# Key and value sums of the projections stage: every second chunk, two chunks together

## The chip, the cores and the metric

The kernel runs on one core of one Trainium2 chip. The metric is the device time of one execution in microseconds (us). Before the change the median of three runs is 2619.73 us (2617.83 to 2623.37).

A core has several engines that run at once and wait for one another through counters (semaphores): TensorE (PE) multiplies matrices, VectorE (DVE) and ScalarE (ACT) work on elements and empty TensorE's results, GpSimd (POOL) works on elements too, SyncE (SP) issues transfers (DMA).

## The reference

The input is 8 images of 256 channels and 64 x 64 positions. Two residual layers follow one another, each behind a group norm:

```python
x = x + window_mixing(group_norm(x))           # 8x8 windows, 16 heads
x = x + attention(group_norm(x))

def attention(x):                              # 256 channels, groups of 8
    qkv  = w_qkv @ x                           # 768 x 256, at each position
    y    = grouped_1x1(depthwise_5x5(qkv))
    q, k, v = heads(concat(qkv, y))            # q = relu(q), k = relu(k)
    v    = pad_with_ones(v)                    # a ninth row, for the denominator
    vk   = sum over positions of v * k         # per image and head: 9 x 8
    out  = (vk @ q)[:8] / ((vk @ q)[8] + 1e-15)
    return batch_norm(w_proj @ out)
```

The change touches the sum `vk` for the heads that come straight from `qkv`, before any convolution.

## The kernel before

The kernel has four stages, one after the other, with a barrier of all engines between them: window mixing, projections, convolved heads, output. The change is in `projections`.

**What a chunk is.** The stage goes through the 8 images; each image is cut into 8 chunks of 512 positions (`n` from 0 to 7), so there are 64 chunks. For each chunk TensorE makes six products `product(b, n, j)` (line 1056). Each is one block of 128 of the 768 output channels, and six matmuls, since operands are split into a high and a low part (`xh`, `xl`, `wh`, `wl`). The products write three PSUM banks in turn (`o_ps`). Products 0 and 2 are blocks of keys, which ACT copies to `kv` (line 976); 1 and 3 are values, copied to `kv` by DVE (line 1201); 4 and 5 are queries, copied to `qw` by ACT (line 1004) and DVE (line 1236).

**Turning and summing.** For the sum over positions, positions must lie on the partitions. `turn(b, n, u)` transposes the key and value tiles of half `u` on TensorE (line 1070), ACT takes the result into `kT` and `vT` (lines 981 and 984), and `sum_vk(b, n, u)` (line 1082) multiplies them: 16 small matmuls of 128 x 32 by 33 columns, each of which the trace shows as two, so 32 for a half and 64 for a chunk. They add up in the bank `vk_ps` over all 8 chunks of an image. The 64 of a chunk stand at its very end, behind product 5; I call them a burst.

**What else TensorE waits for.** The first matmul of a chunk waits for the split of the chunk's input: ACT normalises (`xn`, line 907) and rounds to `xh` (line 917), DVE subtracts to `xl` (line 1148). It also waits for the copies that free its banks. DVE's order in a chunk is: copy of values, two subtractions for the stores (lines 1154 to 1160), those of the queries of the chunk before, second copy of values, two more subtractions, the split `xl` for the next chunk, the copy of queries (line 1236). In chunks 1 to 4 of all images but the last it then adds the statistics of the next image (line 111); after chunk 4 it puts them together (line 120), and in chunk 5 TensorE averages them over groups, between products 1 and 2 (line 158).

**Stores.** DVE and POOL write the differences and the odd columns to `stage`, and SP stores it: six transfers of 408 KB and two of 256 KB a chunk. `stage` has two sets by chunk. At the end of an image ACT starts the load of the image after next, 4096 KB.

**Order in the code.** Each engine runs its own program. `over_image_pairs` writes images 0 and 1 out, runs a loop twice over images 2 to 5, and writes images 6 and 7 out. In the loop, the values of waits are computed in registers; in the written-out code they are constants.

Of the kernel before, what the change touches and what calls it, by code (L numbers as in the profile page):

```python
# [29 lines left out]
P = 128  # L30
# [30 lines left out]
SQ = 32  # L61
# [610 lines left out]
def projections(nc, K, x1_dram, qkv_dram, qr_dram, w_pw, bn_in, taps_dram, sorted_dram):  # L672
# [3 lines left out]
    with ExitStack() as ctx:  # L676
# [21 lines left out]

        kv = sb("kv", [P, 2, 4, 512])
        qw = sb("qw", [P, 2, 2, 512])  # L700
        kT = sb("kT", [P, 2, 4, P])
        vT = sb("vT", [P, 2, 4, NSQ, VS])
        tick = sb("ptick", [P, 4 * NCH])
        pw_rep = sb("pw_rep", [P, QT, NPH, D])
        diag = sb("pdiag", [P, 2, SQ])
# [119 lines left out]

        @block.gpsimd
        def _(pool):
            pool.memset(vT[:, :, :, :, SQ:VS], 1.0).then_inc(zeroed, 1)

            def body(i, last_body):  # L830
                for par in range(2):
                    b = 2 * i + par

                    def pause(k, n):

                        k = NCH * k + n
                        pool.tensor_tensor(tick[:, k:k + 1], K["ident"][:, 0:1], K["ident"][:, 1:2], ALU.add)  # L837

                    def border(n):

                        row = NB * (1 - n // 4)
                        keys_values_free(pool, b, n)
                        queries_free(pool, b, n)
                        pause(0, n)
                        pool.memset(stage[:, n % 2, :, :, :, row, :].rearrange("p t a k x -> p (t a) k x"), 0.0)\
                            .then_inc(bordered, 1)

                    def edge(buf, t0, j0, n):

                        if n % 2:  # L850
                            pool.tensor_scalar(staged(j0, n, 0, 0, 1), every_second(buf, t0, n, 0, 1), -1.0, None, ALU.mult)
                        else:
                            pool.tensor_copy(staged(j0, n, 1, HALF - 1, HALF), every_second(buf, t0, n, NB - 1, 1))

                    def keys_values(n, u):
                        g = NCH * b + n
                        pool.wait_ge(kv_ready, 2 * g + u + 1)
                        pool.wait_ge(kv_ready_v, 2 * g + u + 1)
                        keys_values_free(pool, b, n)
                        pause(1 + u, n)  # L860
                        edge(kv, 2 * u, 2 * u, n)
                        pool.tensor_copy(staged(2 * u, n, 2), every_second(kv, 2 * u, n, 1 - n % 2)).then_inc(kv_odd, 1)

                    def queries(n, end=False):
                        g = NCH * b + n
                        pool.wait_ge(q_ready, g + 1)
                        pool.wait_ge(q_ready_v, g + 1)
                        queries_free(pool, b, n)
                        at_least(pool, K["qr_stored"][n % 2], 32 * (4 * b + n // 2))
                        pause(3, n)  # L870
                        edge(qw, 0, 4, n)
                        pool.tensor_copy(staged(4, n, 2), every_second(qw, 0, n, 1 - n % 2)).then_inc(q_odd, 1)
                        if end:
                            return
                        for t in range(2):
                            last = pool.tensor_scalar(qs[:, n % 2, t, :], qw[:, n % 2, t, :], 0.0, None, ALU.max)  # L876
                        last.then_inc(qs_ready, 1)

                    for n in range(NCH):
                        if n % 4 < 2:  # L880
                            border(n)
                        keys_values(n, 0)
                        if n > 0:
                            queries(n - 1)
                        keys_values(n, 1)
                    queries(NCH - 1, last_body and par == 1)
            over_image_pairs(pool, body)

        @block.scalar
        def _(act):  # L890
# [72 lines left out]
            def body(i, last_body):  # L963
                for par in range(2):
                    b = 2 * i + par
                    for n in range(NCH):
# [10 lines left out]

                        def turned(u):
                            act.wait_ge(t_full, 4 * g + 2 * u + 1)
                            at_least(act, vk_full, g)  # L980
                            act.activation(kT[:, u, :, :].rearrange("p a c -> p (a c)"), t_ps[:, 0, :], ACT.Relu)\
                                .then_inc(k_turned, 1)
                            act.wait_ge(t_full, 4 * g + 2 * u + 2)
                            act.activation(vT[:, u, :, :, 0:SQ].rearrange("p a q c -> p (a q) c"),
                                           t_ps[:, 1, :].rearrange("p (a c) -> p a c", c=SQ), ACT.Copy).then_inc(v_turned, 1)
                        key(0)
                        if last_body and par == 1 and n == 0:
# [35 lines left out]
        def _(pe):  # L1023
# [50 lines left out]
            def sum_vk(b, n, u):  # L1074
                pe.wait_ge(k_turned, 2 * (NCH * b + n) + u + 1)
                pe.wait_ge(v_turned, 2 * (NCH * b + n) + u + 1)
                if n == 0:
                    at_least(pe, vk_taken, 2 * b)
                for a in range(4):
                    for q in range(NSQ):  # L1080
                        ch = slice(SQ * q, SQ * q + SQ)
                        last = pe.matmul(vk_ps[ch, u, 0:VS], kT[:, u, a, ch], vT[:, u, a, q, :],
                                         start=(n == 0 and a == 0), stop=(n == NCH - 1 and a == 3))
                if u == 1:
                    last.then_inc(vk_full, 1)

            def turn_pointwise(step):
# [8 lines left out]
            def body(i, last_body):  # L1096
                for par in range(2):
                    b = 2 * i + par
                    for n in range(NCH):
                        pe.wait_ge(xh_ready, NCH * b + n + 1)  # L1100
                        pe.wait_ge(xl_ready, NCH * b + n + 1)
                        means = variances = None
                        if n == 5 and not (last_body and par == 1):
                            means, variances = norm_group_sums(pe, b + 1, T, mv, stat_ps, K["gavg"], ns)
                        product(b, n, 0)
                        product(b, n, 1)
                        if means:
                            means()
                        product(b, n, 2)
                        turn(b, n, 0)  # L1110
                        if last_body and par == 1 and n in (0, NCH - 1):
                            turn_pointwise(n // (NCH - 1))
                        product(b, n, 3)
                        product(b, n, 4)
                        if variances:
                            variances()
                        turn(b, n, 1)
                        product(b, n, 5)
                        for u in range(2):
                            sum_vk(b, n, u)  # L1120
            over_image_pairs(pe, body)

        @block.vector
        def _(dve):
# [64 lines left out]
            def body(i, last_body):  # L1189
                for par in range(2):  # L1190
# [56 lines left out]
                        if nxt and n == 6:  # L1247
                            scale()
                    queries(NCH - 1)
                    dve.wait_ge(vk_full, NCH * (b + 1))  # L1250
                    at = bass.ds(image(i, par), 1)
                    dve.tensor_tensor(diag[:, :, :], vk_ps[:, :, 0:SQ], K["sqmask"][:, :].unsqueeze(1).broadcast_to([P, 2, SQ]),
                                      ALU.mult).then_inc(vk_taken, 1)
# [903 lines left out]
```

## Time and profile before

| what | value |
|---|---|
| median of the runs | 2619.73 us |
| profiled execution, span from the first to the last instruction | 2613.5 us |
| its own time beside its span | not given apart; the median of the runs is 6.2 us above the span |
| PE busy over the whole span | 2464.0 us (94%) |
| DVE, ACT, POOL busy | 2045.9, 1577.8, 1133.2 us |
| projections stage, about | 366 to 1112 us |
| one chunk, in the written-out code and in the loop | 10.9 and 11.1 us, where nothing holds it up |

The span is cut into stages by their lines. Within the stage the timeline shows each instruction with its start and its duration. Matmuls are pipelined: their durations overlap, so the distance from start to start tells what one costs. An entry in square brackets is idle time of the engine before the instruction, with what ended it.

### The profile page before, as it was taken

Reading aid. Unit: us, or ns where it says so; the run is one execution under the profiler, and the core shown is the slowest. Engines: PE = TensorE matmul, PEld = TensorE weight load, DVE = VectorE, ACT = ScalarE, POOL = GpSimd, SP = SyncE. Lnnn points to the kernel's source line nnn. Section 1 sums busy time; section 2 is a strip of 40 time slices with the busy share of each in tenths; the row PEclk is TensorE's granted clock in tenths of the full one; section 3 lists DMA queues with packets and bytes.
Section 4 is the critical chain, followed back from the end, with each engine's and each line's share of the span. In section 5 each row is a group of like instructions: output and inputs, shape, how many; then the busy total and the mean of one; then the engine's idle time right before and its main releaser. Section 6 shows DMA issues by size and latency. Waiting matters only on the chain. (4 is left out here: it accounts for less than half of the span.)

```text
span 2613.5 us, 62159 instructions
## 1 busy us (share of the span) xinstructions
PE 2464.0 (94%) x22829; PEld 1891.7 (72%) x22829; DVE 2045.9 (78%) x2869; ACT 1577.8 (60%) x2144; POOL 1133.2 (43%) x1631
## 2 busy tenths in 40 slices
PE   5888889999999999979999999999999979999998
PEld 4666667777778778767777777777777746666665
DVE  7777668778877877788888888888888767887885
ACT  5888855666556666666666666666666534334343
POOL 7732327878768777800000000000000048888887
PEclk9999999999999999989999999999999989999999
DMA  7655238888888898998888888888888777777774
GB/s 264 254 199 209 110 113 306 324 321 290 314 311 292 294 334 301 302 243 205 200 199 204 199 199 204 200 199 205 199 198 204 207 241 280 281 277 272 262 270 129
DMA packets 300327, 628.28 MB, mean 240 GB/s; under 512 B 50656, under 2 KB 248032, under 8 KB 294752
## 3 DMA queue, kind: packets, MB, share of 16 engines
q1 hardware_dynamic: 295072, 590.90, 73.5%
q10 hardware_dynamic: 4048, 31.11, 3.3%
q0 software_dynamic: 1008, 3.67, 0.4%
q8 instruction: 118, 1.93, 0.3%
q14 instruction: 81, 0.66, 0.1%
HBM read 327.81 MB, written 300.94 MB: 241 GB/s over the span
## 5 line engine op out<-in xcount | busy, mean ns | idle before, releaser
L1834 POOL TENSOR_TENSOR ql<-image,qh 128x1024 fp32r<-128x1024 f32 x128 | 306.1, 2423 | 999.0 <-ACT qh L1862 999.0
L1490 PE MATMUL c_ps<-dh,wh 128*128 128x512 f32 x1152 | 474.1, 412 | 14.5 <-DVE wl L1640 13.2
L1402 ACT ACTIVATE dh<-image 128x1632 fp32r<-128x1632 f32 x192 | 301.3, 1569 | 277.8 <-PE c_ps L1490 261.2
L1490 PE MATMUL c_ps<-dh,wl 128*128 128x512 f32 x1152 | 454.1, 394 | 0.0
L1490 PE MATMUL c_ps<-dl,wh 128*128 128x512 f32 x1152 | 452.5, 393 | 0.0
L1598 DVE TENSOR_TENSOR dl<-image,dh 128x1632 fp32r<-128x1632 f32 x192 | 355.9, 1854 | 59.8 <-ACT dh L1402 59.8
L1056 PE MATMUL o_ps<-xh,wqh 128*128 128x512 f32 x768 | 320.3, 417 | 11.1 <-issue 7.9
L1056 PE MATMUL o_ps<-xl,wqh 128*128 128x512 f32 x768 | 304.4, 396 | 0.0
L1056 PE MATMUL o_ps<-xh,wql 128*128 128x512 f32 x768 | 303.1, 395 | 0.0
L1490 PEld LDWEIGHTS c_ps<-dh,wh 128*128 128x128 f32 x1152 | 217.0, 188 | 70.5 <-DVE wl L1640 13.3
L1490 PEld LDWEIGHTS c_ps<-dl,wh 128*128 128x128 f32 x1152 | 216.5, 188 | 51.8
L1490 PEld LDWEIGHTS c_ps<-dh,wl 128*128 128x128 f32 x1152 | 217.1, 188 | 40.2
L976 ACT ACTIVATE kv<-o_ps 128x512 f32<-128x512 f32 x128 | 76.8, 600 | 268.5 <-PE o_ps L1056 252.2
L876 POOL TENSOR_SCALAR qs<-qw 128x512 f32<-128x512 f32 x126 | 235.9, 1889 | 0.0
L1883 ACT ACTIVATE zs<-z_ps,bn_shift 128x512 f32<-128x512 f32 x64 | 44.0, 687 | 283.2 <-PE z_ps L1970 283.2
L1970 PE MATMUL z_ps<-qh,fh 128*128 128x512 f32 x512 | 208.7, 408 | 5.7 <-POOL ql L1834 4.0
L1970 PE MATMUL z_ps<-qh,fl 128*128 128x512 f32 x512 | 201.0, 393 | 0.0
L1970 PE MATMUL z_ps<-ql,fh 128*128 128x512 f32 x512 | 200.4, 392 | 0.0
L1201 DVE COPY kv<-o_ps 128x512 f32<-128x512 f32 x128 | 87.8, 686 | 123.9 <-PE o_ps L1056 121.9
L1056 PEld LDWEIGHTS o_ps<-xh,wqh 128*128 128x128 f32 x768 | 146.2, 190 | 39.7 <-issue 14.1
L837 POOL TENSOR_TENSOR ptick<-ident 128x1 f32<-128x1 f32 x224 | 93.4, 417 | 179.9 <-DMA qkv_scratch<-stage 77.2
L1056 PEld LDWEIGHTS o_ps<-xl,wqh 128*128 128x128 f32 x768 | 146.1, 190 | 32.6
(209 smaller groups left out, 5387.5 us busy)
## 6 DMA issues: line engine op xcount, KB each, us to landing
qkv_scratch<-stage SPq DMA_DIRECT2D x384, 408.0 KB, 4.1
image<-qkv_scratch SPq DMA_DIRECT2D x189, 816.0 KB, 6.3
qr_scratch<-qs SPq DMA_DIRECT2D x128, 256.0 KB, 3.2
yq_scratch<-qy SPq DMA_DIRECT2D x64, 512.0 KB, 6.8
image<-qr_scratch SPq DMA_DIRECT2D x128, 256.0 KB, 6.3
image<-yq_scratch SPq DMA_DIRECT2D x128, 256.0 KB, 5.7
ox<-x_scratch SPq DMA_DIRECT2D x8, 4096.0 KB, 15.1
out<-ox SPq DMA_DIRECT2D x7, 4096.0 KB, 12.7
```

The source lines that it names most:

```text
L837: pool.tensor_tensor(tick[:, k:k + 1], K["ident"][:, 0:1], K["ident"][:, 1:2], ALU.add)
L876: last = pool.tensor_scalar(qs[:, n % 2, t, :], qw[:, n % 2, t, :], 0.0, None, ALU.max)
L976: act.activation(kv[:, n % 2, 2 * u, :], o_ps[:, (2 * u) % 3, :], ACT.Copy).then_inc(kv_ready, 1)
L1056: last = pe.matmul(o_ps[:, j % 3, :], w[:, ct, P * t:P * t + P], xx[:, n % 2, ct, :], start=(k == 0), stop=(k == 5))
L1201: dve.tensor_copy(kv[:, n % 2, 2 * u + 1, :], o_ps[:, (2 * u + 1) % 3, :]).then_inc(kv_ready_v, 1)
L1402: act.activation(dh[kind][:, :], raw[kind], ACT.Copy).then_inc(hi_ready, 1)
L1490: last = pe.matmul(c_ps[:, bank(hp, j, kind, m), :], w[hp][:, kind, part, o:o + P], cells[:, :, HALF * dy:HALF * dy + HALF * NB], start=(k ...
L1598: dve.tensor_tensor(dl[kind][:, :], raw[kind], dh[kind][:, :].bitcast(F32), ALU.subtract)\
L1834: pool.tensor_tensor(two_of(ql, n, tp), two(n, tp), two_of(qh, n, tp).bitcast(F32), ALU.subtract)\
L1883: act.activation(zs[:, :], z_ps[:, 1, :], ACT.Identity, bias=bn["shift"][:, 1:2]).then_inc(z_taken, 1)
L1970: last = pe.matmul(z_ps[:, o, :], w[par][:, t, P * o:P * o + P], d, start=(m == 0), stop=(m == 3 * KT - 1))
```

## The change

`kT` and `vT` get a second set, picked by the chunk's parity (`n % 2`). TensorE leaves out the sums at the end of chunks 0, 2, 4 and 6, and does them at the end of chunks 1, 3, 5 and 7, for the chunk before and for the chunk itself: 128 small matmuls in a row. The counter `vk_full` goes up once for two chunks, and those who wait for it, ACT before it writes `kT` and DVE at the image's end, count accordingly. The amount of arithmetic is the same. The burst's place and size are all that moves on TensorE; ACT, DVE, POOL and SP keep their order.

```diff
-        kT = sb("kT", [P, 2, 4, P])
-        vT = sb("vT", [P, 2, 4, NSQ, VS])
+        kT = sb("kT", [P, 2, 2, 4, P])
+        vT = sb("vT", [P, 2, 2, 4, NSQ, VS])
...
-                            at_least(act, vk_full, g)
-                            act.activation(kT[:, u, :, :].rearrange("p a c -> p (a c)"), t_ps[:, 0, :], ACT.Relu)\
+                            at_least(act, vk_full, (NCH // 2) * b + n // 2)
+                            act.activation(kT[:, n % 2, u, :, :].rearrange("p a c -> p (a c)"), t_ps[:, 0, :], ACT.Relu)\
...
-                        last = pe.matmul(vk_ps[ch, u, 0:VS], kT[:, u, a, ch], vT[:, u, a, q, :],
+                        last = pe.matmul(vk_ps[ch, u, 0:VS], kT[:, n % 2, u, a, ch], vT[:, n % 2, u, a, q, :],
                                          start=(n == 0 and a == 0), stop=(n == NCH - 1 and a == 3))
-                if u == 1:
+                if u == 1 and n % 2 == 1:
                     last.then_inc(vk_full, 1)
...
                         product(b, n, 5)
-                        for u in range(2):
-                            sum_vk(b, n, u)
+                        if n % 2 == 1:
+                            for m in (n - 1, n):
+                                for u in range(2):
+                                    sum_vk(b, m, u)
...
-                    dve.wait_ge(vk_full, NCH * (b + 1))
+                    dve.wait_ge(vk_full, (NCH // 2) * (b + 1))
```

On TensorE, the end of chunk 2 of the first image and the start of chunk 3, in the kernel before (`xl_ready` is the split that DVE makes, `v_turned` and `k_turned` are ACT's copies):

```order
L1056 MATMUL o_ps<-xl,wqh 128x512
L1082 MATMUL vk_ps<-vT,kT 32x33 [waits v_turned,k_turned]
L1082 MATMUL vk_ps<-vT,kT 32x33 x15
L1082 MATMUL vk_ps<-vT,kT 32x33 [waits v_turned,k_turned]
L1082 MATMUL vk_ps<-vT,kT 32x33 x15
L1056 MATMUL o_ps<-xh,wqh 128x512 [waits kv_ready_v,q_ready,xl_ready,xh_ready]
```

The same place now:

```order
L1056 MATMUL o_ps<-xh,wqh 128x512
L1056 MATMUL o_ps<-xh,wql 128x512
L1056 MATMUL o_ps<-xl,wqh 128x512
L1056 MATMUL o_ps<-xh,wqh 128x512 [waits kv_ready_v,q_ready,xl_ready,xh_ready]
L1056 MATMUL o_ps<-xh,wql 128x512
```

The first matmul of chunk 3, with its wait for the split, follows product 5 of chunk 2 directly.

On TensorE, the end of chunk 3 now (it had the same rows as the end of chunk 2 before):

```order
L1056 MATMUL o_ps<-xl,wqh 128x512
L1082 MATMUL vk_ps<-vT,kT 32x33 [waits v_turned,k_turned]
L1082 MATMUL vk_ps<-vT,kT 32x33 x15
L1082 MATMUL vk_ps<-vT,kT 32x33 [waits v_turned,k_turned]
L1082 MATMUL vk_ps<-vT,kT 32x33 x15
L1082 MATMUL vk_ps<-vT,kT 32x33 [waits v_turned,k_turned]
L1082 MATMUL vk_ps<-vT,kT 32x33 x15
L1082 MATMUL vk_ps<-vT,kT 32x33 [waits v_turned,k_turned]
L1082 MATMUL vk_ps<-vT,kT 32x33 x15
```

The sums of two chunks stand in a row, with one switch from the large matmuls and one back.

## Rows read from the trace of the kernel before

**Rows 1.** Windows, projections stage: busy PE, PEld, DVE, ACT, POOL; clock, DMA, GB/s.
```profile
366.00:1112.00 746.00, 715.89 (x7458) 583.66 (x7458) 577.26 (x880) 454.65 (x658) 570.42 (x763) 0.98 0.86 302
```

**Rows 2.** Groups by line, projections stage, the sums (line 1082).
```profile
L1082 PE MATMUL vk_ps<-vT,kT 128*32 128x33 f32 x4096 | 49.9, 200 | 1.3 <-ACT vT L984 1.3
```

**Rows 3.** Timeline of PE, end of chunk 4, loop (start us, duration us, ...).
```profile
611.13 0.40 PE L1056 MATMUL o_ps<-xh,wql 128*128 128x512 f32 x1
611.36 0.40 PE L1056 MATMUL o_ps<-xl,wqh 128*128 128x512 f32 x1
611.69 0.77 PE L1082 MATMUL vk_ps<-vT,kT 128*32 128x33 f32 x64
...
612.61 0.47 PE L1056 MATMUL o_ps<-xh,wqh 128*128 128x512 f32 x1
612.91 0.39 PE L1056 MATMUL o_ps<-xh,wql 128*128 128x512 f32 x1
...
615.81 0.38 PE L158 MATMUL pstat_ps<-pmv,gavg 128*128 128x2 f32 x2 [0.24 <-DVE pmv L120]
```

**Rows 4.** Timeline of DVE beside Rows 3.
```profile
610.87 1.21 DVE L1148 TENSOR_TENSOR xl<-xn,xh 128x1024 fp32r<-128x1024 f32 x1
612.01 0.67 DVE L1236 COPY qw<-o_ps 128x512 f32<-128x512 f32 x1
612.61 2.45 DVE L111 BATCH_NORM_STATS2 pbst<-image 128x6 f32<-128x512 f32 x4
...
615.17 0.59 DVE L120 BATCH_NORM_AGGREGATE pmv<-pbst 128x2 f32<-128x48 f32 x2
```

**Rows 5.** Timeline of DVE and PE, end of a chunk 2, unrolled code.
```profile
497.94 1.22 DVE L1148 TENSOR_TENSOR xl<-xn,xh 128x1024 fp32r<-128x1024 f32 x1
...
498.56 0.39 PE L1056 MATMUL o_ps<-xl,wqh 128*128 128x512 f32 x1
...
499.60 0.47 PE L1056 MATMUL o_ps<-xh,wqh 128*128 128x512 f32 x1
```

**Rows 6.** Timeline of DVE and PE, end of a chunk 2, loop.
```profile
871.35 1.22 DVE L1148 TENSOR_TENSOR xl<-xn,xh 128x1024 fp32r<-128x1024 f32 x1
...
871.68 0.40 PE L1056 MATMUL o_ps<-xl,wqh 128*128 128x512 f32 x1
...
872.92 0.47 PE L1056 MATMUL o_ps<-xh,wqh 128*128 128x512 f32 x1
```

**Rows 7.** Timeline of DVE and PE, end of a chunk 0, loop.
```profile
844.82 1.22 DVE L1148 TENSOR_TENSOR xl<-xn,xh 128x1024 fp32r<-128x1024 f32 x1
...
845.57 0.40 PE L1056 MATMUL o_ps<-xl,wqh 128*128 128x512 f32 x1
```

**Rows 8.** Timeline, DVE and PE, chunk 1, the wait on stores.
```profile
853.80 0.63 DVE L1154 TENSOR_TENSOR stage<-kv 128x448 f32<-128x448 f32 x1 [3.08 <-DMA qkv_scratch<-stage]
...
856.91 1.48 PE L1070 MATMUL pt_ps<-ident,kv 128*128 128x128 f32 x8 [2.12 <-DVE kv L1201]
```

**Rows 9.** Timeline of ACT and PE, chunk 6 of the last image.
```profile
1097.13 0.59 ACT L1004 ACTIVATE qw<-o_ps 128x512 f32<-128x512 f32 x1
...
1098.85 0.46 PE L1082 MATMUL vk_ps<-vT,kT 128*32 128x33 f32 x32 [1.27 <-ACT vT L984]
1099.24 0.50 PE L1056 MATMUL o_ps<-xh,wqh 128*128 128x512 f32 x1
```

**Rows 10.** Timeline of DVE and SP's queue, end of the stage.
```profile
1113.88 0.22 DVE L1252 TENSOR_TENSOR pdiag<-vk_ps,sqmask 128x64 f32<-128x64 f32 x1
...
1115.92 2.30 SPq L798 DMA_DIRECT2D qr_scratch<-qs  x2
```

**Rows 11.** Timeline of DVE, the same subtraction twice in one chunk.
```profile
840.52 0.65 DVE L1160 TENSOR_TENSOR stage<-kv 128x448 f32<-128x448 f32 x1
...
843.80 1.10 DVE L1160 TENSOR_TENSOR stage<-kv 128x448 f32<-128x448 f32 x1
```

**Rows 12.** Timeline of PE, start of the loop's second turn.
```profile
743.93 0.77 PE L1056 MATMUL o_ps<-xh,wqh 128*128 128x512 f32 x1 [4.44 <-issue]
```

More of the change, by code:

```diff
@@ L827, in _ @@
         def _(pool):
-            pool.memset(vT[:, :, :, :, SQ:VS], 1.0).then_inc(zeroed, 1)
+            pool.memset(vT[:, :, :, :, :, SQ:VS].rearrange("p m u a q c -> p (m u a) q c"), 1.0).then_inc(zeroed, 1)
             def body(i, last_body):
@@ L979, in turned @@
                             act.wait_ge(t_full, 4 * g + 2 * u + 1)
-                            at_least(act, vk_full, g)
-                            act.activation(kT[:, u, :, :].rearrange("p a c -> p (a c)"), t_ps[:, 0, :], ACT.Relu)\
+                            at_least(act, vk_full, (NCH // 2) * b + n // 2)
+                            act.activation(kT[:, n % 2, u, :, :].rearrange("p a c -> p (a c)"), t_ps[:, 0, :], ACT.Relu)\
                                 .then_inc(k_turned, 1)
                             act.wait_ge(t_full, 4 * g + 2 * u + 2)
-                            act.activation(vT[:, u, :, :, 0:SQ].rearrange("p a q c -> p (a q) c"),
+                            act.activation(vT[:, n % 2, u, :, :, 0:SQ].rearrange("p a q c -> p (a q) c"),
                                            t_ps[:, 1, :].rearrange("p (a c) -> p a c", c=SQ), ACT.Copy).then_inc(v_turned, 1)
```

## The prediction

> **What bounds the kernel now.** I read the page first, for the stage that the change touches, then the stage by windows, then TensorE's timeline at the ends of chunks, and beside it DVE's. In the projections stage PE is busy 715.9 of 746 us, DVE 577.3, ACT 454.7, POOL 570.4, and the DMA share is 0.86 [rows 1]. So TensorE bounds the stage by its own work, and the reader should ask of each end of a chunk: if TensorE gets there earlier, what does it find ready?
>
> The burst of 64 sum matmuls costs little [rows 2, 3]. Matmuls of the products start 0.23 us apart (611.13 to 611.36). Product 5 ends its last start at 611.36, so without a burst the next product could start at 611.59. It starts at 612.61, and its second matmul follows after 0.30 instead of 0.23. The burst of chunk 4 in the loop thus costs 612.61 - 611.59 + 0.07 = 1.09 us. In code that is written out it costs less: 499.60 - (498.56 + 0.23) = 0.81, with the same slow start 0.88 [rows 5]. The difference of 0.2 lies behind the burst, where TensorE works out the values of its waits in registers with no matmul queued that would hide it. A burst takes 0.77 us from its first start to its last end, and one small matmul 0.20, so the 64 starts span 0.57; another 64 behind them cost 0.58. The other 0.30 (written out) or 0.51 (loop) is the way in and out.
>
> **What the change saves if nothing else is late.** 32 ways in and out go, 16 in each kind of code: 16 x 0.30 + 16 x 0.51 = 13.0 us. This is the optimistic sum, and I do not forecast it, since a second half of the change works against it: the burst at the end of an even chunk also covers the split that the next chunk needs.
>
> **What the burst covers.** DVE's split ends at 610.87 + 1.21 = 612.08 in chunk 4, 0.49 us behind the moment at which product 5 leaves TensorE free [rows 3, 4]. In a chunk 2 of the loop it is 871.35 + 1.22 = 872.57 against 871.68 + 0.23 = 871.91: late by 0.66 [rows 6]. In a written-out chunk 2 it is 499.16 against 498.79: late by 0.37 [rows 5]. Only in chunk 0 it is about in time, 846.04 against 845.80, late by 0.24 [rows 7]. DVE begins its series in each of these chunks when product 1 is done, so it moves with TensorE, and the lateness stays when the chunk shifts. Today 1.02 or 0.81 us of burst lie over it and it costs nothing. Without a burst TensorE waits for it, and then pays the hand-over (a few hundredths to 0.1 us, as in rows 3 and 4, where the group average starts 0.05 us after the statistics end at 615.76), in the loop also part of the register work, some 0.2.
>
> **The sum by place in the image.** Savings are in us over all 8 images.
> - Ends of chunks 1, 3 and 5 carry a second 64 matmuls. Nothing lies beside them but what is already waiting, so they are on the path: 24 x 0.58 = 13.9 slower. From below it could be 0.57 less a few hundredths, as the second half has no way in; from above a small matmul that is held up at a lower clock would make it about 0.9 in one or two of them. I take 0.58.
> - End of chunk 7 (+0.58, 7 times, the last image apart) and end of chunk 0 (saves 0.6 to 0.8 written out, about 0.95 in the loop, 7.0 in all) lie between the start of an image's load and the wait for stores that follows in chunk 1 or 2. There DVE waits 3.08 us for a store, and TensorE 2.12 us for DVE [rows 8]. That wait ends when the transfers are through, so what comes before it is given back. Six of eight images have one. Of 4.1 - 7.0 = -2.9 a quarter stays: -0.8. The ends of the range are 0 and -2.9.
> - End of chunk 2: loop 1.02 - 0.66 - 0.26 = 0.1, four times; written out 0.81 - 0.37 - 0.1 = 0.3 at most, three times, with 0.2 as the mean; in the first image, where the chunk follows the wait for stores, the whole 1.1. Together -2.1.
> - End of chunk 4: nothing in seven images. TensorE's next hold is the group average in chunk 5, which begins at 615.81 after 0.24 us of idling, and what it waits for is DVE's series of split, query copy, statistics and aggregation from 610.87 to 615.76 without a gap [rows 3, 4]. No part of that series waits for a burst. TensorE only comes to the wait earlier. The last image has no statistics: -0.3.
> - End of chunk 6: as chunk 2, 0.1 four times in the loop and about 0.3 three times outside: -1.4.
> - End of chunk 6 of the last image: the second half of the burst waited 1.27 us for ACT, which was issuing transfers [rows 9]. Now nothing waits there but product 0 of chunk 7, for ACT's query copy, which ends at 1097.13 + 0.59 = 1097.72. It can start at 1097.8 instead of 1099.24: -1.4.
> - End of chunk 7 of the last image: free. The stage's end goes over DVE's subtractions to SP's last transfers at 1115.92 + 2.30, and DVE takes up the sum only after them, at 1113.88 and without idle time in front [rows 10]; between product 5 and that point it copies, makes the batch norm's scale and two long subtractions, which covers 0.58.
> - ACT's wait before it writes `kT` now asks for the pairs done before the chunk; the last is half a chunk old when ACT gets there. POOL's and SP's order stays. Zero.
>
> Sum: 13.9 - 0.8 - 2.1 - 0.3 - 1.4 - 1.4 = 7.9 us slower. Against the profiled span of 2613.5 this is 2621.4; the median of the runs lies 6.2 above that span, and 2619.7 + 7.9 = 2627.6. As several of the small savings are taken at their lower bound, I put 2627.
>
> **The rule on switching.** The rows show 0.30 to 0.51 us around each burst that is not matmuls of the burst. The Trainium skill ("TensorEngine Tiling (Array Packing)", Key Properties) says that going from one tiling mode to another drains TensorE. Here the products use the whole array and the sums 32 columns of it, so the rule speaks for the change, and by it alone the time would be the optimistic one. The trace agrees that there is a cost at each switch; it does not say that TensorE would find its next input ready.
>
> **Rivals.**
> - *Faster: the split comes in time.* The switches go and TensorE does not wait, but for the average in chunk 5. Then 13.0 is saved less about 1.0 in each of seven chunks 4: -6, giving 2613.5. For it speaks that DVE's split is held back by other work that could shift: the same subtraction before it takes 1.10 us at 843.80 and 0.65 at 840.52 [rows 11]; if it were always the short one, the split would be 0.45 earlier, enough in most written-out chunks and in none of the chunks 2 of the loop (0.66 late). The point from which it decides is a split 0.5 us earlier than now. Against it: the relation of DVE to POOL within an even chunk is set by the same copies as before. The Trainium skill ("SBUF — State Buffer", Who interferes with whom) says that a DVE instruction with two SBUF inputs contends with a GpSimd instruction that reads SBUF, which is how such a shift would act; rows 11 agree with a cost of 0.45 us and cannot tell whose reads cause it.
> - *No change: the waits for stores take it all back.* If transfers set the pace over the whole image (share 0.86), each delay shortens the waits of rows 8, some 2 to 3 us in six images, which are enough for 7.9 in all. Then the time is 2621. Against it: the waits follow the load of 4096 KB and come at the start of an image; the stores of chunks 3 to 6 are through by then.
> - *Much slower: 128 matmuls in a row outrun the supply of instructions.* At the loop's turn TensorE idles 4.44 us for nothing but issue [rows 12]. If each double burst drew 0.5 us of that, 32 x 0.5 = 16 more: 2643. Against it: bursts of 64 show no such gap.
>
> **Chances.** Forecast 0.58, faster 0.12, no change 0.18, much slower or a knock-on late DVE 0.12. A change under 0.2% (5.2 us) cannot be told from none for this kernel. The forecast gives slower with 0.8 of its chance (0.46), as its sum could come out between 3 and 11; with 0.10 of the last rival that is 0.56. Faster is 0.12, and the rest, 0.32, is the same. The range reaches down to the rival without change and some way to the faster one, 2615, and up to a third of the way from the forecast to the last rival and a bit, 2634; about 1 in 10 lies outside on each side. The forecast's own range is 2622 to 2631.
>
> **What would show it.** In the changed profile: bursts of 128, 1.3 to 1.4 us from first start to last end; first products of chunks 3 and 7 of the loop 0.9 to 1.0 us behind product 5's end, with DVE's split named as what ended TensorE's idle time; chunk 5's average at the same distance from chunk 4's start; chunk 7 of the last image starting 1.4 us sooner after chunk 6. Wrong would be a first product that starts at once after chunks 2 and 6 (the faster rival), waits on stores that shrink by the growth of the chunks (the rival without change), or a burst well over 1.4 us (the slower one).

## The result, and the profile after

| kernel | median | lowest to highest | profiled span |
|---|---|---|---|
| before | 2622.09 us | 2617.83 to 2623.87 (5 runs) | 2613.5 us |
| changed | 2642.81 us | 2635.08 to 2645.38 (5 runs) | 2633.3 us |

The ratio is 1.0075, 95% interval [1.0061, 1.009]: 20.7 us slower between the medians, 19.8 between the spans. The forecast was 7.9 slower, and the time lies above the range, at the price of the last rival, 2643. One run of all, the second of the spread kernel's repeat below, was slow (2781.98 us at a granted clock of 0.845 against 0.984 in the first), and no reading uses it.

The projections stage took 757.1 us from its first product to the first convolution matmul of the next stage; now it takes 773.2. Of the 19.8 us these are 16.1; another 2.9 lie before the stage (last section) and 0.8 behind it. The answers to [rows 1, 2], and below them the weight loads and the first matmuls of the products, by lines (busy, mean ns, then idle time with its releasers):

```profile
366.00:1131.00 765.00, 713.07 (x7452) 583.05 (x7452) 580.36 (x885) 457.92 (x662) 569.06 (x764) 0.98 0.84 294
```

```profile
L1082 PE MATMUL vk_ps<-vT,kT 128*32 128x33 f32 x4096 | 46.0, 198 | 8.3 <-issue 8.3
...
L1056 PE MATMUL o_ps<-xh,wqh 128*128 128x512 f32 x768 | 320.3, 417 | 26.8 <-issue 14.1 <-DVE xl L1150 10.5 <-ACT qw L1004 0.7
```

The second line in the kernel before:

```profile
L1056 PE MATMUL o_ps<-xh,wqh 128*128 128x512 f32 x768 | 320.3, 417 | 11.1 <-issue 7.9 <-DVE xl L1148 0.6
```

TensorE is busy no longer than before. Two kinds of idling came: 10.5 us behind DVE's split, which is the end of the even chunks, and "issue": 8.3 us inside the bursts, which [rows 2] did not have, and 14.1 in front of the products, most of it behind bursts and at the loop's turn, where it was 7.9. The clock (0.98) and the DMA share (0.84, before 0.86) did not move against it.

**Ends of chunks that went as forecast.** TensorE's timeline at the end of a chunk 1 of the loop, which answers to [rows 3]:

```profile
776.26 0.39 PE L1056 MATMUL o_ps<-xl,wqh 128*128 128x512 f32 x1
776.57 1.39 PE L1082 MATMUL vk_ps<-vT,kT 128*32 128x33 f32 x128
778.16 0.47 PE L1056 MATMUL o_ps<-xh,wqh 128*128 128x512 f32 x1 [0.21 <-issue]
```

The burst of 128 spans 1.39 us, as forecast. The next, a chunk 2 of the loop, TensorE and DVE, which answers to [rows 6]:

```profile
788.06 0.40 PE L1056 MATMUL o_ps<-xl,wqh 128*128 128x512 f32 x1
789.28 0.47 PE L1056 MATMUL o_ps<-xh,wqh 128*128 128x512 f32 x1 [0.83 <-DVE xl L1150]
```

```profile
787.72 1.22 DVE L1150 TENSOR_TENSOR xl<-xn,xh 128x1024 fp32r<-128x1024 f32 x1
788.85 0.68 DVE L1238 COPY qw<-o_ps 128x512 f32<-128x512 f32 x1
```

The split ends at 788.94, 0.65 us behind 788.29, when TensorE was free (forecast 0.66), and the product follows 0.99 behind that point. The burst that lay over it before cost 1.02: nothing is gained. A chunk 4, TensorE, which answers to [rows 3] in the same place:

```profile
614.62 0.40 PE L1056 MATMUL o_ps<-xl,wqh 128*128 128x512 f32 x1
615.70 0.47 PE L1056 MATMUL o_ps<-xh,wqh 128*128 128x512 f32 x1 [0.68 <-DVE xl L1150]
...
619.08 0.38 PE L158 MATMUL pstat_ps<-pmv,gavg 128*128 128x2 f32 x2 [0.40 <-DVE pmv L120]
```

From product 5's last start to the group average it is 619.08 - 614.62 = 4.46 us; before it was 615.81 - 611.36 = 4.45. The wait for the average takes everything. At the end of chunk 6 of the last image, ACT and TensorE, which answers to [rows 9]:

```profile
1116.60 0.59 ACT L1004 ACTIVATE qw<-o_ps 128x512 f32<-128x512 f32 x1
```

```profile
1116.27 0.39 PE L1056 MATMUL o_ps<-xl,wqh 128*128 128x512 f32 x1
1117.34 0.47 PE L1056 MATMUL o_ps<-xh,wqh 128*128 128x512 f32 x1 [0.68 <-ACT qw L1004]
```

The product follows 0.15 us behind ACT's copy (1117.19), as forecast: chunk 7 starts 1.37 us sooner behind chunk 6 than before.

**The pauses.** In or behind about one burst in three TensorE stops with nothing that it waits for. TensorE's timeline at the ends of chunks 7, 9, 31 (the loop's turn, [rows 12]) and 63:

```profile
463.47 1.24 PE L1082 MATMUL vk_ps<-vT,kT 128*32 128x33 f32 x112
465.76 0.33 PE L1082 MATMUL vk_ps<-vT,kT 128*32 128x33 f32 x16 [1.06 <-issue]
...
487.68 1.37 PE L1082 MATMUL vk_ps<-vT,kT 128*32 128x33 f32 x128
489.92 0.47 PE L1056 MATMUL o_ps<-xh,wqh 128*128 128x512 f32 x1 [0.87 <-issue]
...
746.11 1.37 PE L1082 MATMUL vk_ps<-vT,kT 128*32 128x33 f32 x128
754.59 0.77 PE L1056 MATMUL o_ps<-xh,wqh 128*128 128x512 f32 x1 [7.11 <-issue]
...
1127.69 1.28 PE L1082 MATMUL vk_ps<-vT,kT 128*32 128x33 f32 x118
1131.54 0.31 PE L1082 MATMUL vk_ps<-vT,kT 128*32 128x33 f32 x10 [2.57 <-issue]
```

The page says what else moves then. Its queue q8 carries instructions: 118 packets and 1.93 MB in the whole run, 16.4 KB each. 62 of them start in the stage, for 7452 matmuls and as many weight loads: one per 240 records. Set beside the pauses (packet times from the trace's list of transfers, us; from last start before to first start after):

```
chunk  burst from   packet of q8        last start, resumes      resumes after the packet's end
7      463.47       463.14 to 464.37    464.51, 465.76           1.40
9      487.68       487.31 to 488.41    488.85, 489.92           1.51
41     870.38       870.90 to 871.99    871.29, 873.43           1.44
33     776.57       778.77 to 779.90    no stop
```

All 11 pauses in the stage end 1.2 to 1.5 us (2.1 at the loop's turn) after the end of a packet. In nine of them the packet starts before TensorE stops; at the loop's turn and at chunk 63 it starts 4.3 and 0.2 us after TensorE's last start. Where the packet falls elsewhere, as for chunk 33, there is no pause.

That the queue is TensorE's and that a packet is 256 of its instructions can be read from the experiments: the sums made twice add 8192 records of matmuls and loads and 32 packets (150 against 118), bursts of 80 take away 3072 and 12 (106), bursts of 112 take away 1024 and 4 (114).

### The profile page after: what moved, and what is told of

It is laid out like the page before. It is cut to its first block and busy times, and to the rows that moved or that the text cites. A ratio compares the mean times of both kernels' runs of the same rounds, so it can differ in the third digit from the quotient of the medians.

```text
span 2633.3 us, 62157 instructions
## 1 busy us (share of the span) xinstructions
PE 2464.2 (94%) x22829; PEld 1894.4 (72%) x22829; DVE 2046.7 (78%) x2869; ACT 1577.5 (60%) x2144; POOL 1131.8 (43%) x1631
## 3 DMA queue, kind: packets, MB, share of 16 engines
q8 instruction: 118, 1.93, 0.3%
## 5 line engine op out<-in xcount | busy, mean ns | idle before, releaser
L1056 PE MATMUL o_ps<-xh,wqh 128*128 128x512 f32 x768 | 320.3, 417 | 26.8 <-issue 14.1
```

Of the source, the lines that this page charges most:

```text
L1056: last = pe.matmul(o_ps[:, j % 3, :], w[:, ct, P * t:P * t + P], xx[:, n % 2, ct, :], start=(k == 0), stop=(k == 5))
```

## The experiments

In these lists a stop is a distance between two starts on TensorE in or behind a burst that is at least 0.25 us above the normal one. Chunks are counted from 0 to 63 over the images.

**The buffers alone.** The changed kernel with the sums back at the end of each chunk:

```diff
-                        if n % 2 == 1:
-                            for m in (n - 1, n):
-                                for u in range(2):
-                                    sum_vk(b, m, u)
+                        for u in range(2):
+                            sum_vk(b, n, u)
```

> The changed kernel with its two sets of kT and vT, but each chunk's sums at that chunk's end again, in bursts of 64 as in the kernel before. If the order of the sums is the whole cause, the time is that of the kernel before within 3 us (about 2621), with no pause inside a burst. If the larger buffers or their places in SBUF cost something, it is 5 to 20 us above it.

Measured 2619.76 us (10 runs), ratio to the kernel before 0.9987 [0.9977, 0.9997]. The line of the sums, which had 8.3 us of "issue":

```profile
L1082 PE MATMUL vk_ps<-vT,kT 128*32 128x33 f32 x4096 | 49.8, 199 | 1.2 <-ACT vT L984 1.2
```

So the second buffers and ACT's later wait cost nothing. All of the loss belongs to the order of the sums.

**The split earlier.** The changed kernel with DVE's split in front of its last two subtractions in chunks 2 and 6:

```diff
+                        if n in (2, 6):
+                            split(b, n + 1)
                         keys_values(n, 1)
-                        if n < NCH - 1:
+                        if n in (2, 6):
+                            pass
+                        elif n < NCH - 1:
```

> The changed kernel, with DVE's split for chunks 3 and 7 made before the two subtractions of the second key and value pair, instead of after them. Theory of the uncovered split: the 16 gaps behind chunks 2 and 6 (0.5 us in written-out code, about 1.0 in the loop) go to 0 and 0.2, which saves 8 x 0.5 + 8 x 0.8 = 10 us against the changed kernel: about 2632, still 10 above the kernel before, because the pauses inside the bursts stay. Rival, in which TensorE would only wait for something else at that place: 2642, no saving.

Measured 2635.98 (6 runs), ratio 1.0055 [1.0038, 1.0072], by the ratios some 5 us better than the changed kernel, between the two theories (2632 and 2642). Its chunk 2 and the middle of its chunk 3, TensorE and DVE:

```profile
787.88 0.40 PE L1056 MATMUL o_ps<-xl,wqh 128*128 128x512 f32 x1
788.11 0.47 PE L1056 MATMUL o_ps<-xh,wqh 128*128 128x512 f32 x1
...
793.03 1.06 PE L1070 MATMUL pt_ps<-ident,kv 128*128 128x128 f32 x8 [0.59 <-DVE kv L1203]
```

```profile
786.33 1.43 DVE L1150 TENSOR_TENSOR xl<-xn,xh 128x1024 fp32r<-128x1024 f32 x1 [0.67 <-ACT xh L917]
787.68 1.09 DVE L1161 TENSOR_TENSOR stage<-kv 128x512 f32<-128x512 f32 x1
788.70 0.62 DVE L1162 TENSOR_TENSOR stage<-kv 128x448 f32<-128x448 f32 x1
789.24 0.68 DVE L1242 COPY qw<-o_ps 128x512 f32<-128x512 f32 x1
789.84 2.46 DVE L111 BATCH_NORM_STATS2 pbst<-image 128x6 f32<-128x512 f32 x4
792.22 0.67 DVE L1203 COPY kv<-o_ps 128x512 f32<-128x512 f32 x1
```

The product of chunk 3 follows the last one after 0.23 us: the wait was the split. Over the images the ends of chunks 2 and 6 shrink by 15.9 us against the kernel before, where the changed kernel's shrink by 4.1. But DVE idled 0.67 for ACT and is later by as much, and its copy of values now holds TensorE for 0.59 in chunk 3. Chunks 3 and 4 take 5.9 us more. The pauses are there as before: chunks 3, 7, 9, 27, 29, 31, 41, 45, 47, 59, 61, 63. This settles the even ends, and it settles that they are not what makes the kernel slow.

**The instruction stream moved.** The changed kernel with 256 waits that are already met, on TensorE before its first product:

```diff
+            for _ in range(256):
+                pe.wait_ge(zeroed, 1)
```

> The changed kernel with 128 instructions more on TensorE at the start of the stage, each a wait that is met already, which takes under 2 us once. Everything behind them stands half a block of 256 instructions (16384 bytes) further on. Theory of the instruction supply: pauses of 1 us and more inside or right behind a double burst, which in the changed kernel come in chunks 7, 9, 31, 41, 47, 59 and 61, leave most of these chunks and appear in others; each of them still spans a fetch of a block and ends 1.2 to 1.5 us after it; their sum may be anything from 3 to 20 us, so the time is 2630 to 2650. Rival, in which the pauses come from what these chunks wait for (stores, ACT, DVE): the same chunks, the same lengths, 2642 to 2645.

Measured 2647.01 (4 runs), ratio 1.0101 [1.0078, 1.0125]; the first product came at 381.5 us, 12 later. Those 12 belong to the waits, where I had expected under 2: the trace shows them as 128 instructions (TensorE's sequencer has 2226 records where it had 2098), 0.106 us apart. So everything behind them stands 128 instructions, half a packet, further on, as the expectation says. The stage took 771.7. The bursts of chunk 7, which had a pause, and of chunk 17, which had none:

```profile
471.17 1.48 PE L1084 MATMUL vk_ps<-vT,kT 128*32 128x33 f32 x128
```

```profile
586.81 1.28 PE L1084 MATMUL vk_ps<-vT,kT 128*32 128x33 f32 x119
589.36 0.27 PE L1084 MATMUL vk_ps<-vT,kT 128*32 128x33 f32 x9 [1.27 <-issue]
```

The pauses stand at chunks 17, 31, 33, 51, 55 and 63 instead. Apart from the loop's turn and the end, no chunk keeps its pause. The same arithmetic with the same waits for data pauses elsewhere when only the place of instructions in their stream moves. A cause in data or banks would have stayed.

**Longer bursts without the change.** The kernel before, with each chunk's sums made twice (the outputs differ by that): bursts of 128 behind every chunk, and no end without a burst.

```diff
-                        for u in range(2):
-                            sum_vk(b, n, u)
+                        for rnd in range(2):
+                            for u in range(2):
+                                sum_vk(b, n, u, rnd)
```

> The kernel before, with the sums of each chunk made twice, one after the other, so that every chunk ends with a burst of 128 and no split is ever uncovered (numerator and denominator both double). The 64 more matmuls of each of 64 chunks cost 64 x 0.6 = 38 us. Theory of the instruction supply: on top of that pauses in a burst, of up to 1.3 us each, in a fifth to a half of the 64 bursts, and a longer halt at the loop's turn: 12 to 35 us more, 2671 to 2694 in all. Rival without supply pauses: 2660, and no gap over 0.3 us within a burst.

Measured 2685.09 (4 runs), ratio 1.0237 [1.0214, 1.0261]. The line of the sums:

```profile
L1082 PE MATMUL vk_ps<-vT,kT 128*32 128x33 f32 x8192 | 95.6, 198 | 35.4 <-issue 34.0 <-ACT vT L984 1.3
```

The stage grew by 67.6 us. 64 more matmuls behind each of 64 chunks are 64 x 0.58 = 37. The rest are pauses: 29 beside the loop's turn, 0.3 to 3.3 us each and some 40 us in all, and 2.3 more at the turn. Not all of it reaches the stage's time: the waits in chunks 1 and 5, for stores and for the group average, shrink by 9.5, and the last burst's stop of 3.2 is covered. So the pauses need neither the missing burst nor the late split, only 128 in a row.

**How long a burst may be.** Four kernels. The first two leave work out: the last slice, or the last three, of each sum of an even chunk. That makes bursts of 112 and of 80.

```diff
-                for a in range(4):
+                for a in range(4 if n % 2 else 3):      # bursts of 112
...
+                for a in range(4 if n % 2 else 1):      # bursts of 80
```

> The changed kernel, with the last of the four slices of the even chunk's two sums left out, so that a double burst has 112 matmuls (224 instructions with their weight loads) instead of 128 (256, a whole block of the instruction stream); the sums miss an eighth of the positions. The work left out is 32 x 16 matmuls x 9 ns = 4.6 us. Theory of the instruction supply: a block can no longer be used up within a burst, since 32 instructions of it are 16 product matmuls of 0.23 us; no pause inside or behind a burst but that of the loop's turn, so about 9 to 12 us more go, and the time is 2642 - 4.6 - 11 = 2627, still some 4 to 6 above the kernel before. Rival, pauses that do not hang on the length against a block: the pauses stay, 2638.

> The changed kernel with three of the four slices of the even chunk's two sums left out, so that the long bursts have 80 matmuls, 160 instructions; the sums miss three eighths of the positions. What the runs so far show is that TensorE stops when it has taken 180 to 260 instructions since the fetch of the next block began, and goes on 1.2 to 1.6 us after the fetch ends. Then a burst of 160 cannot pause by itself: no pause of over 0.3 us in it or behind it but the loop's turn and where a fetch begins late. Time: the changed kernel less 32 x 48 x 9 ns = 13.8 us less about 11 us of pauses: 2618. Rival, pauses that stay at any length over 64: 2628.

With 112 it was 2632.86 (5 runs), 1.0041 [1.0026, 1.0056], with stops at chunks 3, 11, 31, 37, 47, 55 and 63. With 80 it was 2627.43 (10 runs), 1.0021 [1.0011, 1.0032], with stops at 31, 51, 55, 59 and 63. Both expectations missed: I had held that a burst must come near a whole packet of 256 instructions. One of 80 (160 with its loads) still stops:

```profile
1031.68 0.93 PE L1082 MATMUL vk_ps<-vT,kT 128*32 128x33 f32 x76
1033.81 0.26 PE L1082 MATMUL vk_ps<-vT,kT 128*32 128x33 f32 x4 [1.20 <-issue]
```

The other two do all of the work, in other portions: halves in threes (96 matmuls behind chunks 1, 2, 4 and 5, 128 behind 7, with the split early in chunks 3 and 6), and chunk 0's sums spread (80 behind chunks 1 to 4, 64 behind 5 to 7).

```diff
+        HALVES = {1: (0, 1, 2), 2: (3, 4, 5), 4: (6, 7, 8), 5: (9, 10, 11), 7: (12, 13, 14, 15)}
...
+                        for h in HALVES.get(n, ()):
+                            sum_vk(b, h // 2, h % 2)
```

> The sums in bursts of three halves, 96 matmuls (192 instructions): behind chunk 1 those of chunk 0 and the first half of chunk 1, behind chunk 2 the other three, so again behind 4 and 5, and the last four halves behind chunk 7. DVE's split for chunks 4 and 7 comes before the subtractions, so that TensorE finds it ready where no burst covers it. Theory: 24 switches of 0.30 (written out) or 0.51 us (loop) go, 9.7 us; the bursts of 192 instructions do not pause, those behind chunk 7 (256) pause in two or three of eight images, 1.3 us each; what DVE does later for the early split costs up to 3. About 2621 - 9.7 + 3 + 2 = 2616, faster than the kernel before. Rival, supply pauses already at 192 instructions: 2625 or more.

```diff
+        BURSTS = {1: ((0, 0, 0, 4), (0, 1, 0, 4), (1, 0, 0, 2)),
+                  2: ((1, 0, 2, 4), (1, 1, 0, 4), (2, 0, 0, 4)),
...
+                        for m, u, first, end in BURSTS.get(n, ()):
+                            sum_vk(b, m, u, first, end, n)
```

> A version made from what the traces show. Only chunk 0 has no burst behind it, since only there the split comes in time; its 64 matmuls are spread over the bursts behind chunks 1 to 4, which have 80, 80, 80 and 80 matmuls (160 instructions), and 5 to 7 keep 64. Theory: eight ends of chunk 0 save 6.5 us, as they did in the changed kernel; 64 matmuls elsewhere cost 64 x 9 ns x 8 = 4.6 us, of which a quarter behind chunk 4 is hidden by the wait for the group average; bursts of 160 instructions do not pause. About 3 us less than the kernel before: 2617 to 2618. Rival, that bursts over 64 pause wherever they stand: 2622 or more.

The threes: 2628.39 (9 runs), 1.0025 [1.0015, 1.0035], with eight stops, the longest 3.04 apart from the loop's turn; one behind the burst of 96 of chunk 60 was 1.38. I had expected 2616; it is the rival's time. Spread: 2631.26 (6 runs), 1.0036 [1.0022, 1.0051], a clear miss of the 2617 to 2618 expected. Here the pauses nearly went (chunks 27 and 43 and the loop's turn), but chunks 1 and 2 took 10.5 us more than before. I ran it and the kernel before once more to see whether that was chance.

> The spread sums once more (80, 80, 80, 80, 64, 64, 64 behind chunks 1 to 7). The first trace had 772.3 us for the stage, of which only some 6 were pauses for instructions: chunks 1 and 2 had 10.5 us more of waits for stores than the kernel before. If that belongs to the kernel, it comes back: stage 769 to 775, the bodies of chunks 1 and 2 again 7 us or more above those of the kernel before. If it was chance of one run, the bodies of chunks 1 and 2 come within 4 us of the kernel before and the stage is 761 to 766.

> The kernel before, run once more with a profile, to see what two traces of one kernel differ by. In the first trace the stage took 757.1 us from its first product to the next stage's first matmul, with the only pause of TensorE for instructions at the loop's turn (4.64 us). If instruction fetches are as regular as I hold, there is again no pause over 0.6 us but the loop's turn, 4.5 to 7 us, and the stage takes 755 to 760 us. If pauses of 1 to 2 us also come with bursts of 64, the theory that only longer bursts outrun the fetches falls. The waits for stores in chunks 1 and 2 may differ by up to 4 us in their sum over 8 images; if they differ by 8 or more, the excess of the spread sums is chance.

The kernel before: 2622.23 (8 runs), 0.9996 [0.9983, 1.001]; stage 756.4 us, no stop but the loop's turn (5.22) and the 1.54 that is ACT's. Its turn, which answers to [rows 12]:

```profile
736.85 0.77 PE L1082 MATMUL vk_ps<-vT,kT 128*32 128x33 f32 x64
742.64 0.77 PE L1056 MATMUL o_ps<-xh,wqh 128*128 128x512 f32 x1 [5.02 <-issue]
```

Place by place its two traces differ by less than 0.6 us over the eight images, but for 1.5 in chunk 1. The spread kernel: a single run to compare, 2629.15 us, so no ratio; stage 767.0, 2 us below what was expected, no pause for instructions beyond the loop's turn, and chunks 1 and 2 again 9.0 above the kernel before (10.1 above its second trace). The wait for stores at DVE, summed over the stage, in the kernel before (second trace), the changed kernel, and the spread one (second trace):

```profile
L1154 DVE TENSOR_TENSOR stage<-kv 128x448 f32<-128x448 f32 x64 | 44.0, 688 | 22.2 <-DMA qkv_scratch<-stage 16.9
```

```profile
L1156 DVE TENSOR_TENSOR stage<-kv 128x448 f32<-128x448 f32 x64 | 43.2, 675 | 19.5 <-DMA qkv_scratch<-stage 14.2
```

```profile
L1160 DVE TENSOR_TENSOR stage<-kv 128x448 f32<-128x448 f32 x64 | 43.4, 678 | 28.2 <-DMA qkv_scratch<-stage 22.9
```

Leaving the burst out of chunk 0 brings TensorE to chunk 1 some 0.7 us sooner in each image (5.5 and 6.0 in all), and there it waits for stores by that much longer. That is the rival of the stores, true for this place. The remaining 3 to 5 us of the longer chunks 1 and 2 I cannot explain.

**Sums behind a product.** The kernel with two buffers and a burst of 64 for each chunk, but behind product 0 of the next chunk (chunk 7's stays at its own end), and the split early in chunks 1 to 6:

```diff
                         product(b, n, 0)
+                        if n > 0:
+                            for u in range(2):
+                                sum_vk(b, n - 1, u)
```

> Single bursts as in the kernel before, but behind product 0 of the next chunk instead of in front of it (that of chunk 7 stays), and DVE's splits for chunks 2 to 7 before the subtractions. No burst is longer than 64, so supply gives no pause. What is tested is the 0.2 us of register work that lies bare behind each burst in the loop: behind product 0 it is hidden, if the split is ready by then, which saves 28 x 0.2 = 5.6 us, 2616. If the split is not ready in time, or DVE's later subtractions hold up something else, this is lost: 2621 to 2630.

Measured 2621.63 (11 runs), 1.0006 [0.9997, 1.0015]; no stop but the loop's turn (6.38); the 2616 expected was missed. Each end without a burst shrank by 6.0 to 8.2 us over the eight images, and each middle grew by 5 to 12 with the burst in it and DVE's later copies: the time only changes its place.

**The changed kernel again**, with its stream untouched:

> The changed kernel once more. If the pauses come from where the bursts stand in the instruction stream, they are in the same chunks as in its first trace (7, 9, 25, 29, 31, 41, 45, 47, 59, 61, 63), give or take the small ones; if they come from chance in the transfers, they are elsewhere. The start of the first product tells how much of the time differs from run to run before the stage begins.

Measured 2643.03 (2 runs), 1.0086 [1.0065, 1.0108]. TensorE at the end of chunk 7:

```profile
464.95 1.24 PE L1082 MATMUL vk_ps<-vT,kT 128*32 128x33 f32 x112
466.97 0.33 PE L1082 MATMUL vk_ps<-vT,kT 128*32 128x33 f32 x16 [0.78 <-issue]
```

It stops behind the same 112th record. The chunks with stops are 7, 9, 29, 31, 41, 45, 47, 59, 61 and 63, as in the first trace, and 3 and 27 besides; chunk 25 is missing. The places repeat, a few at the margin come and go.

## Why the prediction was wrong

The 63 steps from one chunk's first product to the next one's, the changed kernel against the kernel before (first trace), in us over all images. The time of a pause (what its distance has over the usual one at such a place: 0.01 us within a burst, 0.16 behind one in the written-out code, 0.35 in the loop, at the loop's turn the 4.64 of before) is taken out of its place and stands in a row of its own.

| step of the prediction | forecast | changed | changed again |
|---|---|---|---|
| ends of chunks 1, 3, 5 | +13.9 | +13.2 | +13.5 |
| ends of chunks 7 and 0, and the waits on stores in chunks 0 to 2 | -0.8 | -6.3 | -2.9 |
| end of chunk 2 | -2.1 | -1.6 | -1.6 |
| end of chunk 4 with chunk 5's average | -0.3 | +0.4 | -0.4 |
| end of chunk 6 (-1.4 in the last image among it) | -2.8 | -2.5 | -2.6 |
| middles of chunks 3, 4, 6, 7 | 0 | +0.1 | +0.8 |
| sum | +7.9 | +3.4 | +6.8 |
| pauses for instructions | 0 | +11.8 | +15.2 |
| all 63 steps | +7.9 | +15.2 | +22.0 |

Chunk 63 adds 0.9 and 1.9, and little of it comes from its burst. That is stopped for 2.6 us, but DVE takes up the sum at 1132.00, 14.66 us after the chunk's first product (1117.34); before it was 14.64, and 14.84 in the repeat. So the sum is still covered, as forecast [rows 10], though by no more than 0.15 us and not at all in the repeat. The rest comes behind it, where SP's last transfers start 0.9 and 1.9 us later than before; why is open.

- **What failed is the step of the last rival.** I took the pauses at nothing in the sum and gave them a chance of 0.12, because "bursts of 64 show no such gap". That was an inference from 64 to 128 without a reason why the cost should not begin in between. It does: none of the kernels with bursts of 64 stops outside the loop's turn (three kernels, four traces), and those of 80 do now and then, of 112 and 128 often. It is not that packets miss the bursts of 64: in the first trace of the kernel before, 19 of them start between 0.6 us in front of a burst's first matmul and 0.5 behind it. One lies over the burst of [rows 3], from 611.16 to 612.21, and nothing stops. The sign that the prediction named for this rival, a burst well over 1.4 us, is in the trace: 2.4 us from first to last start at chunk 7. The rival's total, 2643, is what was measured, but partly by luck: 2.9 of the 20.7 us lie before the stage, and its working was another. It had 32 pauses of 0.5 us, and there are 10 or 11 of 0.35 to 3.0 and a loop's turn longer by some 2.6.
- **The clue was in the trace before.** The loop's turn [rows 12] showed that TensorE can be left without instructions. The queue of instruction packets stood in the page; I had not set it beside TensorE's timeline. 63 packets in 757 us are one in 12 us, in plain work; a double burst uses up 256 instructions in 1.2 us, one packet takes 0.96 us (median) to arrive, and TensorE went on only 1.2 to 1.5 us behind that. The first two figures stood in the trace before, and would have moved the chance; the third only the pauses show.
- The Trainium skill ("Advanced Engine Details and Errata", ISA Cache) gives a cache line of 16 KB, 256 instructions. The packets here are of that size, 16.4 KB. That section says nothing of a stop when they run out, nor for how long.
- **The sum without pauses.** It came to 3.4 and 6.8 against 7.9. The second 64 matmuls cost 0.60 us at most places (1.17 from first to last start against 0.57), 0.55 and 0.56 in the mean of the 24. The split's lateness and the average's distance came out within 0.02 us. The rule on switching was no guide to the time: the ways in and out went, and the split was not ready.
- **The waits for stores shrank where the forecast had them grow.** Ends of chunks 7 and 0 alone are +4.3 and -6.5, near the forecast (+4.1 and -7.0). Three quarters of the 2.9 saved were to come back as longer waits, 2.1; but the middles of chunks 0 to 2 shrank by 4.1 in the first trace and 1.5 in the second. The pauses at chunk 7 (4.9 and 4.5 us) come just in front of these waits, so part of their time is taken back there: that step of the sum was wrong too, because it had no pauses. How much is taken back differs by 2.6 us between two traces of the same kernel. (Two small terms of the forecast are 0.1 too large: a quarter of 2.9 is 0.7, and the ends of chunk 6 add up to 1.3. It changes nothing.)
- **No rival of gain.** The splits never came in time except behind chunk 0, where I had it late by 0.24 and it was not late: 764.71 + 1.33 = 766.04 against 766.20.

```profile
764.71 1.33 DVE L1150 TENSOR_TENSOR xl<-xn,xh 128x1024 fp32r<-128x1024 f32 x1
```

What is shown: the pauses move with the stream (the 256 waits), repeat with it, come with the length of the bursts alone (sums made twice), and are absent at 64. What is not: what exactly TensorE holds in advance, and what decides when a packet starts. From the packet's start to the resumption TensorE took some 125 to 260 records, and 70 and 77 where the packet started late (chunk 57 of the threes, chunk 41 here). At chunk 63, and at 16 and 56 with the sums made twice, the packet started only after TensorE had stopped. I have no rule that names each of them.

No kernel here beats the one before by a margin that matters; the two buffers with bursts of 64 come nearest (0.9987).

## What to carry over

Before putting short instructions in a row, compare two times: how long the row takes to use up a packet's instructions (1.2 us for 256 here), and how long it is from a packet's start until the engine goes on (2.2 to 3.0 us in the changed kernel's pauses within and behind bursts). Here rows that used 160 instructions or more in one go stopped in some places, which depend on everything in front of them in the stream. And ask of a burst what it covers: of the four places in an image where a burst was taken away, only chunk 0 gave its time back (6.5 us). Behind chunks 2, 4 and 6 most of it went, because the next input was late by nearly as much as the burst had taken.

## What the runs showed of the hardware

- TensorE stopped for 0.3 to 3.3 us in or behind rows of 80 to 128 small matmuls (with their loads 160 to 256 instructions, 9 ns per matmul). It resumed 1.2 to 1.6 us after the end of an instruction packet of 16.4 KB, which itself took 0.97 us in the changed kernel (median, 0.88 to 1.9) and 0.96 in the kernel before.
- The second turn of the loop cost 4.6 and 5.2 us of TensorE before, 6.2 with bursts of 64 and two buffers, 7.2 and 7.3 in the changed kernel, 7.7 with the 256 waits, and 4.6 in one trace of the spread kernel, 6.8 in the other.
- 256 waits that were already met, in one row, are 128 instructions in the trace, 0.106 us apart. They delayed the stage's first product by 12 us against the changed kernel (369.5 to 381.5).
- That first product came at 366.6 and 366.5 us in the two traces of the kernel before, at 369.5 and 368.0 in those of the changed one, and at 368.4 in the one with the old buffers and doubled sums. With two buffers it was 366.6 where the split is earlier and 370.1 with bursts of 80. Nothing in front of it was changed, but for the places of buffers; the cause is open.
